# Batch statistics behind the first batch's keys and query, and 16 filler transposes in place of 24, at the start of a gated cross-attention kernel

## The chip, the cores and the metric

The kernel runs on one core of one Trainium2 chip. Its engines are TensorE (PE in the profile, with its weight loads as PEld), VectorE (DVE), ScalarE (ACT), GpSimd (POOL) and SyncE (SP), which issues most DMAs. The metric is the device time of one execution in microseconds; less is better.

## What is computed

Two layers over 8 batches of 112 query tokens of width 256, with 375 context tokens for each batch. Layer 0 is a gated cross-attention with 16 heads of 16, a layer norm for each head on queries and keys, and a feed-forward of three chained matrices; layer 1 is a cross-attention with 8 heads of 64 and a mixture of eight experts. The part that the change lies in is the beginning of layer 0:

```python
x = x + jnp.tanh(g_xattn[0]) * _L0_xattn_ref(_layernorm(x, axis=-1), ctx_1024, Wq, Wkv, Wp, bp, ln_g, ln_b)
# in _L0_xattn_ref
q = (x_query @ Wq).reshape(B, Nq, H, D).transpose(0, 2, 1, 3)
kv = (x_context @ Wkv).reshape(B, Nc, 2, H, D)
q = layernorm(q, ln_g, ln_b)
k = layernorm(k, ln_g, ln_b)
attn = jax.nn.softmax(jnp.einsum('bhqd,bhkd->bhqk', q * SCALE, k), axis=-1)
```

## The kernel before

All five engines run lists of stages that one function, `attention_order`, makes: tables give each stage a due time (in no unit that is measured), all stages are sorted by it, and each engine walks the sorted list and issues the stages that are its own. An engine runs its instructions in that order and waits on semaphores for what other engines deliver. So a changed due time can change the place of a stage on its own engine, and nothing else. The table `FIRST` holds the stages of batches 0 and 1 at the start of layer 0.

Stages that matter here, by the name in the table, the engine and the line of the instruction:

- `stats0` b (VectorE, L1208 and L1210): mean and variance of batch b's tokens, two instructions, BN_STATS and BN_AGGR.
- `rs0` (GpSimd, L2077 into `ve` and L2079 into `rstd`): variance plus epsilon, then the power -1/2. Piece 0 is batch 0; piece 1 is batches 1 and 2 in one instruction each, so it waits for the statistics of both; piece 2 is batches 3 to 7.
- `norm` b (VectorE, L1257): the normalised tokens `XN`; `xt` b (TensorE, L593): their transposes, two of them; `xtc` (ScalarE, L1735) copies them into `XT`.
- `kp` (TensorE, L566, and L610 for the query): products of context and tokens with the key and query weights. One such product in the code is two matmuls in the trace. `kq` (ScalarE, L1801 and L1802): squares into `sq` and the plain copy into `kraw`, which empties the PSUM bank.
- `kss` (VectorE, L1264): sums of squares by head; for batch 0 it is followed by twelve small instructions on VectorE (L1480 to L1491) that find the inverse roots.
- `ksc` (VectorE, L1285): `kraw` times the roots into `KN`, two of them for batch 0; the second holds key third 2 and the query. `qaff` (L1457, VectorE for batch 0) adds the shift to the query.
- `spk` b, j (TensorE, L635, four transposes) turns key third j; `spq` (L643) turns the query. `spkc` (L1523 on VectorE for thirds 0 and 1, L1521 on ScalarE for third 2) and `spqc` (ScalarE, L1820) copy them to `KT0` and `QA0`.
- `S0` q (TensorE, L656): score products of quad q (four heads of one batch), eight matmuls in the trace; `max0` (VectorE, L1295): row maxima; `qt2` (TensorE, L664) and `st` (L674): scores once more, turned; `ex` (ScalarE, L1834): the exponential.
- `v` (TensorE, L566) and `vc` (ScalarE, L1810, into `V`): value products and their copies.

Three PSUM banks are handed round between these products (`take` waits for the copy that empties one): the transposes `spk` 0, 2 need the first of them, `spk` 0, 0 the one that batch 1's first `kq` empties, and `spk` 0, 1 the one that `spkc` 0, 2 empties. The first `kq` of batch 1 may start when the first `ksc` of batch 0 has read `kraw`.

`WARM` names stages ahead of which TensorE runs fillers: transposes of the identity (L559) whose results nobody reads. Ahead of `spk` 0, 2 there are 24.

GpSimd fills buffers (`fill`: `V01`, `KN1`, `ZT`, from 14.09 us on) ahead of piece 1 of `rs0`.

Of the kernel before, what the change touches and what calls it, by code (L numbers as in the profile page):

```python
# [15 lines left out]
NB, NQ, NC, D = 8, 112, 375, 256  # L16
# [70 lines left out]
def emptied_by(stage, *i):  # L87
# [4 lines left out]
    if stage in ("kp", "v"):  # L92
# [13 lines left out]
        (-8.82, 'spkc', 0, 0), (-11.17, 'spk', 0, 1), (-6.18, 'spkc', 0, 1), (-14.74, 'stats0', 1),  # L106
        (-10.6, 'stats0', 2), (-10.72, 'ksc', 0, 0), (-10.44, 'qaff', 0), (-13.38, 'spk', 0, 2),
        (-11.82, 'spkc', 0, 2), (-12.55, 'spq', 0), (-8.21, 'spqc', 0), (-4.49, 'rs0', 1), (9.09, 'rs0', 2),
        (-17.4, 'kp', 1, 1, 0), (-15.19, 'kp', 1, 1, 1), (-13.03, 'kq', 1, 1), (0.4, 'kss', 1, 1),
        (-7.03, 'norm', 1, 0), (-7.61, 'xt', 1, 0), (-6.84, 'xtc', 1, 0), (-10.64, 'kp', 1, 0, 0),  # L110
        (3.62, 'kp', 1, 0, 1), (5.22, 'kq', 1, 0), (8.46, 'kss', 1, 0), (13.34, 'ksc', 1, 1), (17.76, 'spk', 1, 0),
        (17.28, 'spkc', 1, 0), (19.77, 'spk', 1, 1), (18.91, 'spkc', 1, 1), (11.79, 'ksc', 1, 0), (8.26, 'qaff', 1),
        (18.53, 'spk', 1, 2), (16.36, 'spkc', 1, 2), (14.74, 'spq', 1), (15.82, 'spqc', 1))
# [65 lines left out]


RC, RP = 6, 4
WARM = {("kp", 0, 1, 0): 36, ("spk", 0, 2): 24, ("rt4", NB - 1): 14, ("xin", 0): 62,
        ("up", 0, 0): 10}

WARM_BANK = {("up", 0, 0): 5}
# [121 lines left out]
def build(nc, A, out):  # L307
    ctx = ExitStack()
    with ctx:
# [5 lines left out]
        def s(name):  # L315
            if name not in sems:
                sems[name] = ctx.enter_context(nc.semaphore("s_" + name))
            return sems[name]
# [236 lines left out]
        def keep_warm(e, w, *entry):  # L555

            w.wait_ge(s("pool0"), ID_SET)
            for _ in range(WARM.get(entry, 0)):
                e.transpose(ps[:, WARM_BANK.get(entry, 0), 0:128], ident[:, :], ident[:, :])  # L559
# [1875 lines left out]
```

## Time and profile before

| | |
|---|---|
| median of 3 runs | 568.48 us (568.22 to 568.93) |
| profiled execution | 568.3 us, span 566.5 us |
| TensorE busy | 544.5 us, 96% |
| VectorE busy | 392.0 us, 69% |
| ScalarE busy | 318.9 us, 56% |
| GpSimd busy | 224.6 us, 40% |
| granted TensorE clock, mean | 0.996 |

The time of the profiled execution is 1.8 us above its span, which counts from the first to the last instruction. Times in the rows count from the start of the span. "Busy" of TensorE counts pipelined matmuls from start to end, so that a full row of nines does not mean that the array is at its peak. A row of the timeline gives start, duration, engine, line, operation, what it writes and reads, how many were merged into the row, and in brackets how long the engine was idle before it and what released it. In a row of several, the duration reaches from the start of the first to the end of the last.

### The profile page before, as it was taken

What the parts mean: (1) busy time and instruction counts of PE and PEld (TensorE: products, weight loads), DVE (VectorE), ACT (ScalarE), POOL (GpSimd) and SP (SyncE); (2) the same over time, 40 slices, a digit from 0 to 9 for tenths busy, and PEclk for the clock granted to TensorE, in tenths of its full rate; (3) what the DMA queues carried; (4) which work ended last, traced back from release to release, by engine and by line L of the source; (5) the groups of instructions that cost most, each with busy time, mean ns of one, the idle gap of its engine ahead of it and who ended that gap; (6) DMA issues with size and microseconds to landing.
All of it is one profiled execution on the core that took longest, in us unless ns stands there. A gap on an engine that the chain in (4) does not pass through costs nothing.

```text
span 566.5 us, 13539 instructions
## 1 busy us (share of the span) xinstructions
PE 544.5 (96%) x5530; PEld 469.4 (83%) x5530; DVE 392.0 (69%) x764; ACT 318.9 (56%) x629; POOL 224.6 (40%) x239
## 2 busy tenths in 40 slices
PE   8999999999999999999999999999799998999994
PEld 7776767777767878988898888888799996999994
DVE  7887567687778757668765756667676774677752
ACT  3454545655656565666656665556556574567631
POOL 3568549558560134235233432412311333042432
PEclk9999999999999999999999999999999999999998
DMA  8920670000000000000000000007682577177111
GB/s 248 337 94 2 252 311 3 1 3 1 2 2 2 1 1 2 2 9 26 5 23 10 18 17 10 26 1 303 218 276 60 206 262 247 22 256 264 19 12 24
DMA packets 22971, 50.66 MB, mean 89 GB/s; under 512 B 6464, under 2 KB 15728, under 8 KB 19568
## 3 DMA queue, kind: packets, MB, share of 16 engines
q1 hardware_dynamic: 18208, 44.94, 22.2%
q0 software_dynamic: 3456, 3.69, 3.6%
q10 hardware_dynamic: 1232, 1.01, 0.7%
q8 instruction: 49, 0.80, 0.6%
q14 instruction: 26, 0.21, 0.1%
HBM read 37.63 MB, written 12.52 MB: 89 GB/s over the span
## 4 chain that ended last, share of the span: by engine, by line
PE 79%; POOL 8%; DVE 6%; issue 3%; DMA 2%; ACT 1%; POOLq 0%; DVEq 0%
PE ps L65 16%; PE ps L67 15%; PE ps L66 15%; POOL sr L2097 6%; PE ps L799 5%; PE ps L817 5%; PE ps L787 5%; PE ps L656 4%; PE ps L674 3%; DVE KN L1295 3%; PE ps L690 2%; PE ps L635 2%; PE ps L920 1%; PE ps L593 1%; ACT P L1834 1%
## 5 line engine op out<-in xcount | busy, mean ns | idle before, releaser
L2097 POOL TENSOR_TENSOR sr<-sv,mhalf 125x32 f32<-125x32 f32 x13 | 70.6, 5433 | 1.1
L65 PE MATMUL ps<-XGf,WH 128*128 128x256 f32 x252 | 71.0, 282 | 0.0
L66 PE MATMUL ps<-XGf,WH 128*128 128x256 f32 x252 | 71.0, 282 | 0.0
L67 PE MATMUL ps<-XGf,WL 128*128 128x256 f32 x252 | 70.8, 281 | 0.0
L1295 DVE TENSOR_REDUCE KN<-ps 112x4 f32<-112x1500 f32 x32 | 55.0, 1719 | 18.6 <-PE ps L656 18.2
L1710 DVE TENSOR_TENSOR WL<-WR,WH 128x1024 fp32r<-128x1024 f32 x48 | 57.1, 1220 | 12.8 <-ACT WH L2054 8.5
L2170 POOL TENSOR_SCALAR P<-P,rinv 112x487 f32<-112x487 f32 x56 | 40.7, 738 | 56.3 <-DVE rinv L1338 55.3
L1899 ACT ACTIVATE P<-ps,nm 112x487 f32<-112x487 f32 x64 | 42.0, 664 | 23.6 <-DVE nm L1330 23.6
L1834 ACT ACTIVATE P<-ps 125x1344 f32<-125x1344 f32 x32 | 41.4, 1293 | 22.7 <-PE ps L674 22.2
L464 POOL DMA_INDIRECT out<-WS,rows_i x16 | 28.6, 1790 | 62.1 <-ACT WS L1988 46.4
L2054 ACT ACTIVATE WH<-WR 128x1024 fp32r<-128x1024 f32 x48 | 48.8, 1051 | 0.1
L65 PEld LDWEIGHTS ps<-XGf,WH 128*128 128x128 f32 x252 | 47.4, 188 | 0.4 <-issue 0.4
L66 PEld LDWEIGHTS ps<-XGf,WH 128*128 128x128 f32 x252 | 47.4, 188 | 0.0
L67 PEld LDWEIGHTS ps<-XGf,WL 128*128 128x128 f32 x252 | 47.4, 188 | 0.0
L65 PE MATMUL ps<-HTf,CS 128*125 128x256 f32 (+1 forms) x120 | 44.5, 371 | 0.0
L1636 DVE TENSOR_TENSOR P<-P,ps 128x512 f32<-128x512 f32 x32 | 21.9, 686 | 31.2 <-PE ps L67 30.6
L1330 DVE TENSOR_REDUCE nm<-ps 112x1 f32<-112x487 f32 x64 | 38.2, 656 | 4.0 <-PE ps L787 4.0
L1973 ACT ACTIVATE P<-ps 128x512 f32<-128x512 f32 x32 | 19.1, 595 | 37.7 <-PE ps L67 35.7
L67 PE MATMUL ps<-HTf,CS 128*125 128x256 f32 (+1 forms) x120 | 39.2, 327 | 0.0
L65 PE MATMUL ps<-WH,HTf 128*128 128x256 f32 x128 | 36.9, 288 | 0.0
L66 PE MATMUL ps<-WL,HTf 128*128 128x256 f32 x128 | 36.0, 282 | 0.0
L67 PE MATMUL ps<-WH,HTf 128*128 128x256 f32 x128 | 36.0, 281 | 0.0
(302 smaller groups left out, 1502.9 us busy)
## 6 DMA issues: line engine op xcount, KB each, us to landing
WR<-in_gupT SPq DMA_DIRECT2D x16, 1024.0 KB, 7.8
WR<-in_dwnT SPq DMA_DIRECT2D x8, 1024.0 KB, 11.2
xs<-ZT SPq DMA_DIRECT2D x14, 516.0 KB, 6.8
CT<-in_ctxT SPq DMA_DIRECT2D x1, 2250.0 KB, 12.0
P<-xs SPq DMA_DIRECT2D x7, 256.0 KB, 10.5
Wk<-in_L_xattn_Wk SPq DMA_DIRECT2D x2, 512.0 KB, 11.2
Wv<-in_L_xattn_Wv SPq DMA_DIRECT2D x2, 512.0 KB, 11.6
out<-X SPq DMA_DIRECT2D x8, 112.0 KB, 1.9
```

What stands on the lines that cost most here:

```text
L65: e.matmul(out, ah, bh, start=start, stop=False)
L66: e.matmul(out, ah, bl, start=False, stop=False)
L67: return e.matmul(out, al, bh, start=False, stop=stop)
L464: return e.indirect_dma_start(result, rows, src, None, bounds_check=NT - 1, oob_is_err=False, compute_op=ALU.add)
L1295: e.tensor_reduce(heads(KN[b % 2][0:NQ, 3, :])[:, 4 * k:4 * k + 4, 16], ps[0:NQ, 0:4, 0:NC], AX.X, ALU.max, negate=True).then_inc(s("smax" ...
L1330: e.tensor_reduce(nm[:, k:k + 1], ps[0:NQ, scores_bank(*i) + z, 0:487], AX.X, ALU.max, negate=True).then_inc(s("nm"), 1)
L1710: e.tensor_tensor(WL[x % 3][:, cs], WR[x % 3][:, cs], f_(WH[x % 2][:, cs]), ALU.subtract).then_inc(s("wl"), 1)
L1834: e.activation(PQ[:, q % 3, :].rearrange("p (g n) -> p g n", g=4), ps[0:125, 0:4, 0:3 * NQ], ACT.Exp).then_inc(s("ex"), 1)
L1899: e.activation(P[:, k, 0:487], ps[0:NQ, scores_bank(*i) + z, 0:487], ACT.Exp, bias=nm[:, k:k + 1], accum_out=rsum[:, k:k + 1] if i[0] < LA ...
L2054: e.activation(WH[x % 2][:, cs], WR[x % 3][:, cs], ACT.Copy).then_inc(s("wh"), 1)
L2097: e.tensor_tensor(sr[:, p, :], sv[:, p, :], mhalf[0:125, 0:32], ALU.pow).then_inc(s("sr"), 1)
L2170: e.tensor_scalar(P[:, k, 0:487], P[:, k, 0:487], rinv[:, k:k + 1], 1.0, ALU.mult, ALU.mult).then_inc(s("psc"), 1)
```

## The change

Four due times in `FIRST` and one count in `WARM`:

```diff
-        (-8.82, 'spkc', 0, 0), (-11.17, 'spk', 0, 1), (-6.18, 'spkc', 0, 1), (-14.74, 'stats0', 1),
-        (-10.6, 'stats0', 2), (-10.72, 'ksc', 0, 0), (-10.44, 'qaff', 0), (-13.38, 'spk', 0, 2),
+        (-8.82, 'spkc', 0, 0), (-11.17, 'spk', 0, 1), (-6.18, 'spkc', 0, 1), (-10.3, 'stats0', 1),
+        (-8.0, 'stats0', 2), (-10.72, 'ksc', 0, 0), (-10.44, 'qaff', 0), (-13.38, 'spk', 0, 2),
...
-        (-7.03, 'norm', 1, 0), (-7.61, 'xt', 1, 0), (-6.84, 'xtc', 1, 0), (-10.64, 'kp', 1, 0, 0),
+        (-6.1, 'norm', 1, 0), (-6.05, 'xt', 1, 0), (-6.84, 'xtc', 1, 0), (-10.64, 'kp', 1, 0, 0),
...
-WARM = {("kp", 0, 1, 0): 36, ("spk", 0, 2): 24, ("rt4", NB - 1): 14, ("xin", 0): 62,
+WARM = {("kp", 0, 1, 0): 36, ("spk", 0, 2): 16, ("rt4", NB - 1): 14, ("xin", 0): 62,
```

No stage is added or removed, and what each stage does stays the same.

On VectorE, between the last root step of batch 0 and the first row maximum, this stood before (`ksc` is L1285, `qaff` L1457, `stats0` L1208 and L1210, `spkc` L1523, `norm` L1257):

```order
34 L1208 BN_STATS st<-X 112x6
35 L1210 BN_AGGR mv<-st 112x2
36 L1285 TENSOR_TENSOR KN<-kraw,sr 125x32x16 x2
37 L1208 BN_STATS st<-X 112x6
38 L1210 BN_AGGR mv<-st 112x2
39 L1457 TENSOR_TENSOR KN<-KN,S 112x16x16
40 L1523 COPY KT<-ps 128x4x125
41 L1257 TENSOR_SCALAR XN<-X,mv,rstd 112x256
42 L1523 COPY KT<-ps 128x4x125
43 L1257 TENSOR_SCALAR XN<-X,mv,rstd 112x256
44 L1295 TENSOR_REDUCE KN<-ps 112x4
```

and now, in the same place on VectorE:

```order
34 L1285 TENSOR_TENSOR KN<-kraw,sr 125x32x16 x2
35 L1457 TENSOR_TENSOR KN<-KN,S 112x16x16
36 L1208 BN_STATS st<-X 112x6
37 L1210 BN_AGGR mv<-st 112x2
38 L1523 COPY KT<-ps 128x4x125
39 L1208 BN_STATS st<-X 112x6
40 L1210 BN_AGGR mv<-st 112x2
41 L1523 COPY KT<-ps 128x4x125
42 L1257 TENSOR_SCALAR XN<-X,mv,rstd 112x256 x2
43 L1295 TENSOR_REDUCE KN<-ps 112x4
```

Both scalings and the query shift have moved ahead of the statistics of batch 1, the statistics of batch 2 have moved behind the first key copy, and `norm` of batch 1 behind the second.

On TensorE, ahead of the transposes of batch 0's keys, only the number of fillers (L559) differs:

```order
 L610 MATMUL ps<-WS,XT 112x256 x2
 L566 MATMUL ps<-WS,CT 125x256 x10
-L559 MATMUL ps<-ident 128x128 x24
+L559 MATMUL ps<-ident 128x128 x16
 L635 MATMUL ps<-ident,KN 128x125 x8
 L643 MATMUL ps<-ident,KN 128x112 x4
```

Nothing else moves there: `xt` of batch 1 still stands between the key product of batch 1 and the score product of quad 0. The lists of ScalarE, GpSimd and SyncE are as before.

## Rows read from the trace of the kernel before

**Rows 1.** The page, chain that ended last: shares of the span by engine.
```profile
PE 79%; POOL 8%; DVE 6%; issue 3%; DMA 2%; ACT 1%; POOLq 0%; DVEq 0%
```

**Rows 2.** Timeline of TensorE, 15 to 45 us: start us, us, engine, line, operation, idle before.
```profile
15.71 2.78 PE L559 MATMUL ps<-ident 128*128 128x128 f32 x24
18.33 1.02 PE L635 MATMUL ps<-ident,KN 125*128 125x125 f32 x8
...
19.60 0.65 PE L635 MATMUL ps<-ident,KN 125*128 125x125 f32 x4
20.12 1.13 PE L566 MATMUL ps<-WS,CT 128*125 128x256 f32 x4
21.09 0.36 PE L593 MATMUL ps<-ident,XN 112*128 112x112 f32 x2
21.37 0.90 PE L656 MATMUL ps<-KT,QA 32*112 32x375 f32 x8
...
24.12 0.32 PE L664 MATMUL ps<-ident,KN 112*128 112x112 f32 x1 [0.40 <-DVE KN L1295]
```

**Rows 3.** Timeline of VectorE, the same stretch.
```profile
15.87 0.23 DVE L1491 SCALAR_TENSOR_TENSOR sr<-S,sr 125x64 f32<-125x64 f32 x1
16.01 0.42 DVE L1208 BATCH_NORM_STATS2 st<-X 112x6 f32<-112x256 f32 x1
...
16.57 1.27 DVE L1285 TENSOR_TENSOR KN<-kraw,sr 125x512 f32<-125x512 f32 x2
17.76 0.42 DVE L1208 BATCH_NORM_STATS2 st<-X 112x6 f32<-112x256 f32 x1
18.21 0.18 DVE L1210 BATCH_NORM_AGGREGATE mv<-st 112x2 f32<-112x6 f32 x1
18.31 0.41 DVE L1457 TENSOR_TENSOR KN<-KN,S 112x256 f32<-112x256 f32 x1
19.39 0.68 DVE L1523 COPY KT<-ps 128x500 f32<-128x500 f32 x1 [0.67 <-PE ps L635]
19.98 0.40 DVE L1257 TENSOR_SCALAR XN<-X,mv,rstd 112x256 f32<-112x256 f32 x1
20.30 0.67 DVE L1523 COPY KT<-ps 128x500 f32<-128x500 f32 x1
...
22.34 1.72 DVE L1295 TENSOR_REDUCE KN<-ps 112x4 f32<-112x1500 f32 x1 [1.05 <-PE ps L656]
```

**Rows 4.** Timeline of GpSimd, the same stretch.
```profile
18.65 0.23 POOL L2077 TENSOR_SCALAR ve<-mv 112x2 f32<-112x2 f32 x1
18.96 0.72 POOL L2079 TENSOR_TENSOR rstd<-ve,mhalf 112x2 f32<-112x2 f32 x1
```

**Rows 5.** Timeline of ScalarE, the same stretch.
```profile
17.35 0.60 ACT L1801 ACTIVATE sq<-ps 125x512 f32<-125x512 f32 x1 [3.65 <-DVE KN L1285]
17.85 0.59 ACT L1802 ACTIVATE kraw<-ps 125x512 f32<-125x512 f32 x1
18.32 0.60 ACT L1810 ACTIVATE V<-ps 125x512 f32<-125x512 f32 x1
18.96 0.59 ACT L1521 ACTIVATE KT<-ps 128x500 f32<-128x500 f32 x1
```

**Rows 6.** Timeline of all engines, 0 to 40 us: batch 0's `rstd` and `norm`.
```profile
8.27 0.57 POOL L2079 TENSOR_TENSOR rstd<-ve,mhalf 112x1 f32<-112x1 f32 x1
...
8.94 0.41 DVE L1257 TENSOR_SCALAR XN<-X,mv,rstd 112x256 f32<-112x256 f32 x1
```

**Rows 7.** Timeline of all engines, 26.5 to 28.1 us.
```profile
26.60 1.37 POOL L2093 TENSOR_SCALAR sv<-ss 125x32 f32<-125x32 f32 x1
26.97 0.93 DVE L1225 TENSOR_TENSOR CS<-CT,CS 128x750 fp32r<-128x750 f32 x1
```

**Rows 8.** L559's transposes 4.6 to 5.6 (ns min/median/max); TensorE in 72 to 76 us (busy, PEclk).
```profile
L559 PE MATMUL ps<-ident x6: 272/392/421, 4.6 to 5.6; 128*128 128x128 f32 x6
...
72.00:76.00 4.00, 3.04 (x47) 1.00 1.03 399
```

## The prediction

> **What bounds the kernel now.** The chain that ended last gives TensorE (PE) 79% of the span, so most of the kernel is matmul work in a row [rows 1]. The change touches neither that work nor the later stages; it touches the stretch from 16 to 22 us, before the first score product of layer 0. There the question is not who is busy but what the first score product (L656, `S0` of quad 0) waits for, because TensorE runs its list in order and everything later stands behind it. So the views to read are the timelines of the four engines in that stretch, one after the other, with the order of the instructions beside them.
>
> TensorE [rows 2]: 24 fillers from 15.71 us, then eight transposes of keys at 18.33 (thirds 2 and 0), the four of the query, four of keys at 19.60 (third 1), the key product of batch 1 at 20.12, the transposes of batch 1's normalised tokens (L593, `xt`) at 21.09, the score product at 21.37. From 20.12 to 21.37 it has no gap: the score product is held by TensorE's own list. VectorE (DVE) [rows 3]: the last root step ends at 15.87 + 0.23 = 16.10; statistics of batch 1 at 16.01; the two scalings of keys at 16.57, together 1.27; statistics of batch 2 at 17.76, done at 18.21 + 0.18 = 18.39; query shift 18.31; a wait of 0.67 for the transposes; key copy 19.39, `norm` of batch 1 at 19.98, key copy 20.30. GpSimd (POOL) [rows 4]: `ve` 18.65 and the power `rstd` 18.96 to 19.68. So the normalisation that `xt` needs had its input at 19.68, stood behind the key copy until 19.98, and was done at 20.38, 0.7 us before TensorE came to `xt`. That is the slack this change draws on.
>
> After the score product comes a tight chain: it ends at 22.27, the row maximum on VectorE runs 22.34 to 24.06, and the next transpose on TensorE starts at 24.12 [rows 2, 3]. A shift of the first score product is therefore expected to go to the end whole, in either direction: what follows waits for each other's results, not for anything that comes at a fixed time.
>
> **The change, part by part.**
>
> Fillers, 24 to 16. One costs (18.33 - 15.71) / 24 = 0.109 us of TensorE's time [rows 2], eight cost 0.87. The sixteen that stay end at 15.71 + 16 x 0.109 = 17.46. The gain is real only as far as the keys are there.
>
> Key scalings ahead of both statistics. The statistics of batch 1 no longer stand between the root and the scalings. With 0.04 from one instruction's end to the next one that waited for it (the wait of 19.35 to 19.39 [rows 2, 3]), the scalings start at 16.14 and end at 16.14 + 1.27 = 17.41, against 17.84: 0.43 earlier. TensorE can start its key transposes at 17.46, just when the sixteen fillers end. The shortened filler is thus sized to the scalings: 0.87 less on TensorE.
>
> Not all of that 0.87 arrives. ScalarE (ACT) frees two PSUM banks here [rows 5]. Its square of batch 1's first key part started 0.78 after the first scaling (17.35 against 16.57), so now at 16.92; the copy `kraw` follows at 17.42 and ends at 18.01; it frees the bank of the second group of transposes. The first four transposes go 17.46 to 17.89, the second four start at 18.05 and end at 18.05 + 0.59 = 18.64 (half of the eight: 1.02 - 4 x 0.107). The copy to `V` moves to 17.89 and the key copy on ScalarE to 18.37, by ScalarE's own pitch of 0.48 (18.53 if it starts only when the copy to `V` has ended); at 18.96 its bank is free, and the last key transposes start at 19.01 instead of 19.60. The key product of batch 1 then starts at 19.53 and TensorE is at `xt` at 19.53 + 0.97 = 20.50 instead of 21.09. By TensorE alone the first score product would be 0.59 earlier.
>
> Statistics behind the key copy. Count VectorE on: query shift 17.45 to 17.86; statistics of batch 1, a pair that takes 0.55 of the engine (17.76 to 18.31 [rows 3]), 17.77 to 18.39, in what was idle time, so they cost nothing; key copy at 18.68 (transposes done 18.64 + 0.04); after 0.59 (19.39 to 19.98) statistics of batch 2 at 19.27, the second half at 19.72, done at 19.90. Before it was 18.39. These statistics were done 1.5 us earlier, and GpSimd's `rs0` takes both batches in one instruction of two columns, so batch 1's `rstd` waits for batch 2's statistics as well. This is the price of the move. From there: hand-over to GpSimd 0.10 (the same that lies between 8.84, the end of the first `rstd`, and 8.94 [rows 6]), `ve` 20.00, `rstd` 0.31 later at 20.31 and 0.72 long to 21.03 [rows 4], hand-over 0.10, `norm` 21.13 to 21.53 (0.40 [rows 3]), hand-over to TensorE 0.05 (24.06 to 24.12), `xt` at 21.58, score product 0.28 later (21.09 to 21.37) at 21.86. Before: 21.37. **The sum is +0.49 us**: +1.08 at `xt` against TensorE's own new time of 20.50, minus the 0.59 won.
>
> What no row shows is the time of `ve` and `rstd` in their new neighbourhood. Lower bound: both hand-overs at 0.04, which takes 0.12 off: +0.37. Upper bound: if the key transposes and the copy each come by the slower reading (ScalarE's key copy at 18.53, hand-overs of 0.10 throughout), +0.7. I take +0.49. The second key copy on VectorE, 19.82 to 20.50, and `norm` of batch 2, behind `norm` of batch 1, lie beside waits and cost nothing. GpSimd's memsets, which end where `ve` starts before (18.65 [rows 4]), don't move and are no longer what it waits for. SyncE, ScalarE and GpSimd keep their lists, and no DMA is moved.
>
> **Against which time.** The profiled run took 568.3 us, 0.2 below the median of 568.48. The sum gives 568.8 for that run and 568.48 + 0.49 = **568.97** for the median. A measurement of this kernel can tell some 0.2% (1.14 us) from no change: below 567.34 is faster, above 569.62 slower. The forecast is no change that can be told, with the sign on the slow side.
>
> **The rivals.**
>
> (a) The gain at the front wins. If `norm` is there by 20.50, the score product starts at 20.78, -0.59: 567.9. For it: TensorE and ScalarE really are earlier, by rows. Against it: `rstd` would have to be done by about 20.0, before the statistics of batch 2 have even been handed over by the working above. It needs an error of a whole microsecond in a chain of five steps, each with a row.
>
> (b) The shift is absorbed: 568.5. For it: there are waits of several engines later on, and the chain has POOL at 8% [rows 1]. Against it: in the stretch behind the score product the wait of one engine is the work of the next.
>
> (c) Slower, by the GpSimd step. The tiny `sv` at 26.60 took 1.37 while `ve`, as small, takes 0.23; VectorE's subtraction into `CS` ran from 26.97 to 27.90 and `sv` ended with it [rows 7, 4]. One engine can hold the other. In the new order `ve` (20.00) falls into VectorE's key copy (19.82 to 20.50), where it did not before. If that copy holds it as the subtraction held `sv`, it costs up to 1.37 - 0.23 = 1.14 on top: +1.63, 570.1. It decides if `ve` is held beyond some 0.65 us more. Against it: the power at 18.96 ran through the start of the same copy at 19.39 and ended at 19.68, with no sign of it.
>
> The Trainium skill bears on (c) (SBUF — State Buffer, Who interferes with whom): the shared port pair is exclusive, a VectorE instruction with two SBUF inputs contends with a GpSimd one that reads SBUF, and one with at most one SBUF input outside the two-port modes doesn't. By that rule the subtraction holds `sv` and the key copy, whose source is PSUM, does not hold `ve`: the trace agrees for both (1.37, and the power that ended at 19.68), and (c) would fall away; its chance is small for the row's reason alone.
>
> (d) Slower, by TensorE's clock. TensorE now idles from about 20.6 to 21.58 and has lost eight fillers, and if the granted clock falls from 1.00 to a half (2.4 to 1.2 GHz), the products behind run at the slow rate: transposes took 421 ns against 272 on either side of the rise at 4.6 to 5.6 us [rows 8]. Over some 2 us of matmul work that doubles, less what waits anyway, +1.5 to +2: about 570.7. Against it: in the stretch 72 to 76 us TensorE was busy for 3.04 of 4.00 us and the granted clock stayed 1.00 [rows 8], and 20 to 24 will be as busy as that.
>
> A page speaks for a free hand with fillers: the Trainium skill (TensorE: Matmul & The Clock Gate, Part 4) says that transposes don't count as work that raises the clock. Then eight fillers fewer could not matter to (d) at all. The trace differs: only transposes had run when they went from 421 to 272 ns, so fillers do raise it and (d) keeps its chance.
>
> (e) The change doesn't do what it says: the list of VectorE does move, as the order shows, so this can only be that the scalings don't start earlier. Then TensorE waits for them where it ran fillers, and the statistics are as late or later: +0.5 to +0.9, inside the range.
>
> **How the numbers follow.** The late normalisation, with (e): 0.62, 568.8 to 569.4. (b): 0.15, 568.5. (a): 0.12, 567.9, with 0.05 of it for something later that gains too and takes it below 567.34. (c): 0.06, 570.1. (d): 0.05, 570.7. Low end: (a) with a little beyond, 567.8. High end: the upper bound of the main case, 568.48 + 0.7, and the 0.35 to 0.45 by which runs of before stood above the lowest or the median: 569.6. Left out are (c), (d) and a tail of (a), some 0.15. Faster 0.05, slower 0.11, same 0.84.
>
> **What the profile after would show.** Right: key scalings at about 16.1; fillers end at 17.5; key transposes at 17.5 with a short gap before the second four; statistics of batch 2 done at 19.9; `rstd` done at 21.0; a gap of about 1 us on TensorE before `xt`, ended by VectorE's `norm`; the first score product at 21.8 to 21.9; the same lateness at 43 and at the end of the span. Wrong: `xt` at 20.5 with no gap (a); the score product late but the last instructions on time (b); `ve` or `rstd` longer than 0.3 or 0.8 (c); a granted clock under 1.00, or transposes of 421 ns, after 20 us (d).

## The result and the profile after

The changed kernel takes 569.36 us (median of 20 runs, 568.5 to 571.12), the kernel before 568.44 in the same comparison (20 runs, 567.9 to 569.87). The ratio is 1.002, 95% interval 1.0012 to 1.0027: slower by 0.7 to 1.5 us. The forecast was 568.97 and a shift of +0.49. The profiled execution has a span of 567.3 us against 566.5. One of the 12 runs of an experiment below (the kernel before with 16 fillers) took 2928.71 us in a slow state and is left out of its ratio.

Every experiment below is read at the same three points, as a distance from the start of the last root step (the second L1491 of batch 0), since that start moved between 15.54 and 16.67 us from one profile to the next, ahead of all that was edited: to the first score product (first L656), to quad 4's (the L656 near 43 us), and from there to the end of the span.

The timelines of after, in the same columns as before. TensorE, answering [rows 2]:

```profile
15.93 1.91 PE L559 MATMUL ps<-ident 128*128 128x128 f32 x16
17.79 1.15 PE L635 MATMUL ps<-ident,KN 125*128 125x125 f32 x8
18.79 0.60 PE L643 MATMUL ps<-ident,KN 112*128 112x112 f32 x4
19.27 0.65 PE L635 MATMUL ps<-ident,KN 125*128 125x125 f32 x4
19.75 1.09 PE L566 MATMUL ps<-WS,CT 128*125 128x256 f32 x4
21.93 0.39 PE L593 MATMUL ps<-ident,XN 112*128 112x112 f32 x2 [1.09 <-DVE XN L1257]
22.25 0.90 PE L656 MATMUL ps<-KT,QA 32*112 32x375 f32 x8
```

VectorE, answering [rows 3]:

```profile
16.09 0.22 DVE L1491 SCALAR_TENSOR_TENSOR sr<-S,sr 125x64 f32<-125x64 f32 x1
16.35 1.29 DVE L1285 TENSOR_TENSOR KN<-kraw,sr 125x512 f32<-125x512 f32 x2
17.68 0.42 DVE L1457 TENSOR_TENSOR KN<-KN,S 112x256 f32<-112x256 f32 x1
18.02 0.42 DVE L1208 BATCH_NORM_STATS2 st<-X 112x6 f32<-112x256 f32 x1
18.48 0.18 DVE L1210 BATCH_NORM_AGGREGATE mv<-st 112x2 f32<-112x6 f32 x1
18.98 0.68 DVE L1523 COPY KT<-ps 128x500 f32<-128x500 f32 x1 [0.32 <-PE ps L635]
19.58 0.42 DVE L1208 BATCH_NORM_STATS2 st<-X 112x6 f32<-112x256 f32 x1
20.03 0.18 DVE L1210 BATCH_NORM_AGGREGATE mv<-st 112x2 f32<-112x6 f32 x1
20.13 0.65 DVE L1523 COPY KT<-ps 128x500 f32<-128x500 f32 x1
21.37 0.73 DVE L1257 TENSOR_SCALAR XN<-X,mv,rstd 112x256 f32<-112x256 f32 x2 [0.60 <-POOL rstd L2079]
23.22 1.72 DVE L1295 TENSOR_REDUCE KN<-ps 112x4 f32<-112x1500 f32 x1 [1.11 <-PE ps L656]
```

GpSimd, answering [rows 4]:

```profile
20.30 0.23 POOL L2077 TENSOR_SCALAR ve<-mv 112x2 f32<-112x2 f32 x1 [1.40 <-DVE mv L1210]
```

ScalarE, the plain copy that frees a PSUM bank, answering [rows 5]:

```profile
17.65 0.59 ACT L1802 ACTIVATE kraw<-ps 125x512 f32<-125x512 f32 x1
```

TensorE by stretches (busy time, matmuls, granted clock, share of the DMA engines, GB/s), with the gap in them:

```profile
19.00:21.00 2.00, 1.84 (x12) 1.00 1.12 274
21.00:23.00 2.00, 1.07 (x10) 1.00 1.12 299
```

Read from the end: the score product follows `xt`, `xt` waited 1.09 us for `norm` (XN L1257), `norm` 0.60 for GpSimd's `rstd`, and GpSimd 1.40 for the statistics of batch 2 (mv L1210). TensorE had ended all that stands ahead of `xt` at 20.84 (21.93 - 1.09), so its own list was indeed ahead. The first score product stands 6.16 us behind the last root step, against 21.37 - 15.87 = 5.50 [rows 2, 3]: **+0.66**. At quad 4 it is 28.01 against 27.35, again +0.66.

### The profile page after: what moved, and what is told of

Its sections match the earlier page's. It is cut to its first block, busy times and chain, and to the rows that moved or that the text cites. A ratio compares the mean times of both kernels' runs of the same rounds, so it can differ in the third digit from the quotient of the medians.

```text
span 567.3 us, 13523 instructions
## 1 busy us (share of the span) xinstructions
PE 544.3 (96%) x5522; PEld 469.3 (83%) x5522; DVE 392.6 (69%) x764; ACT 318.7 (56%) x629; POOL 224.8 (40%) x239
## 3 DMA queue, kind: packets, MB, share of 16 engines
q0 software_dynamic: 3456, 3.69, 3.5%
## 4 chain that ended last, share of the span: by engine, by line
PE 82%; POOL 8%; DVE 6%; issue 2%; ACT 1%; DMA 1%; POOLq 0%
PE ps L65 16%; PE ps L67 15%; PE ps L66 15%; POOL sr L2097 6%; PE ps L799 5%; PE ps L817 5%; PE ps L787 5%; PE ps L656 4%; PE ps L674 3%; DVE KN L1295 3%; PE ps L690 2%; PE ps L635 2%; PE ps L559 2%; PE ps L566 1%; PE ps L920 1%
```

## The experiments

All kernels in one table, in us. Distances come from one profile each; the third column is a span, known to 0.1, less a start. The ratios come from timed runs beside the kernel before. None of them is a difference of 2%; an interval that leaves out 1 shows a direction and little more.

| kernel | first score product | quad 4 | from quad 4 to the end | ratio to before, 95% |
|---|---|---|---|---|
| before | 5.50 | 27.35 | 523.3 | |
| after | 6.16 | 28.01 | 523.2 | 1.002 (1.0012 to 1.0027) |
| after again | 6.15 | 28.01 | 523.5 | 1.0009 (0.9996 to 1.0021) |
| before, 16 fillers | 5.29 | 27.15 | 523.6 | 1.0 (0.9989 to 1.0011) |
| after, 24 fillers | 6.78 | 28.64 | 523.5 | 1.0031 (1.0013 to 1.0049) |
| before, 33 fillers | 6.48 | 28.33 | 523.4 | 1.0018 (1.0003 to 1.0034) |
| after, both statistics first | 5.33 | 27.18 | 523.2 | 0.9998 (0.9989 to 1.0008) |
| after, `rstd` one batch each | 5.47 | 27.33 | 523.5 | 1.0002 (0.9994 to 1.0011) |
| after, `xt` behind the score product | 4.74 | 26.93 | 523.6 | 0.9987 (0.9978 to 0.9996) |
| both statistics first, `xt` behind | 4.77 | 26.78 | 523.4 | 0.9985 (0.9976 to 0.9994) |
| the same again | 4.78 | 26.79 | 523.3 | 0.9989 (0.998 to 0.9998) |
| the same, weight split later | 4.78 | 27.23 | 523.4 | 1.0003 (0.9994 to 1.0013) |
| the same, no fillers there | 4.78 | 26.78 | 526.6 | 1.0044 (1.0026 to 1.0061) |
| the same, the fillers moved to 403 us | 4.78 | 26.78 | 524.9 | 1.0016 (1.0005 to 1.0028) |

### The changed kernel again

No edit; it shows how much of a difference between comparisons is chance.

> The changed kernel once more. In its profile the whole beginning lay 0.2 us later than in the profile before (last root step 16.09 against 15.87), ahead of anything that the change moves; the rest of the lateness of the first score product, 0.67 us, lies behind it. Theory (late normalisation): the offset of the beginning is chance and goes, the distance from the last root step to the first score product stays at 6.1 to 6.2 us (5.50 before), and the kernel is 0.6 to 0.8 us slower than before. Rival (something beyond that stretch also costs): the distance is the same but the kernel is 1.0 to 1.4 us slower.

Measured: the distances repeat to 0.01 us (6.15, 28.01), while the median, 569.02, and the ratio (0.5 us; 0.6 to 0.8 was forecast) are lower than in the first comparison. In the 20 runs of the first, seven lay at 570.2 or above, six of these with a mean granted clock of 0.994 or 0.995 where all the others had 0.996 to 0.998; here two of 12 lay so high, both at 0.994. So the medians carry about half a microsecond that has nothing to do with the order at 16 us, and mechanisms are better read from the distances.

### The two halves of the change, each alone

Only the fillers, on the kernel before:

```diff
-WARM = {("kp", 0, 1, 0): 36, ("spk", 0, 2): 24, ("rt4", NB - 1): 14, ("xin", 0): 62,
+WARM = {("kp", 0, 1, 0): 36, ("spk", 0, 2): 16, ("rt4", NB - 1): 14, ("xin", 0): 62,
```

> The kernel before with 16 fillers in place of 24, its due times as they were. Theory: TensorE is ready at about 17.5 and waits for the key scalings that end at 17.84; the banks that ScalarE empties hold it a little more; the first score product comes 0.1 to 0.3 us earlier than before and the time is 568.2 to 568.4, no difference that can be told. Rival (the fillers carry the clock): the granted clock falls or the transposes go to 421 ns after 16 us, and the kernel is 1 to 2 us slower.

Measured: -0.21 at the first score product, and no difference in time (1.0). Eight fillers, worth 0.87 of TensorE's time, gain only 0.2 as long as the key scalings stand behind the statistics: TensorE idles 0.37 for them. The rival, that the fillers carry the clock, fails here: granted clock 1.00 from 15 to 25 us, transposes of 270 ns.

Only the order, with 24 fillers left (the same line, from 16 back to 24 in the kernel after):

> The changed kernel with 24 fillers: the new order alone. Theory: the fillers hold the key transposes to their old time, the first key copy on VectorE with them, and the statistics of batch 2 behind it end at 20.6; rstd at 21.7, the first score product 1.3 us later than before, 0.6 later than with 16 fillers: 569.7 to 569.9. Rival (the statistics are not what the score product waits for): 568.4 to 569.0.

Measured: +1.28 (1.3 forecast), and 570.03 us. The later transposes push the key copy on VectorE to 19.49, behind it the statistics of batch 2 (20.09 and 20.54), and `ve`, which waits for them:

```profile
19.49 0.68 DVE L1523 COPY KT<-ps 128x500 f32<-128x500 f32 x1 [0.95 <-PE ps L635]
20.09 0.42 DVE L1208 BATCH_NORM_STATS2 st<-X 112x6 f32<-112x256 f32 x1
20.54 0.18 DVE L1210 BATCH_NORM_AGGREGATE mv<-st 112x2 f32<-112x6 f32 x1
...
20.81 0.23 POOL L2077 TENSOR_SCALAR ve<-mv 112x2 f32<-112x2 f32 x1 [2.02 <-DVE mv L1210]
```

The halves don't add (-0.21 and +1.28 against +0.66 together), because in the new order the fillers also set the time of the key copy behind which the statistics stand.

### Does a shift pass to the end?

Nine fillers more than before, 33, cost 0.98 us of TensorE's time and touch nothing else.

```diff
-WARM = {("kp", 0, 1, 0): 36, ("spk", 0, 2): 24, ("rt4", NB - 1): 14, ("xin", 0): 62,
+WARM = {("kp", 0, 1, 0): 36, ("spk", 0, 2): 33, ("rt4", NB - 1): 14, ("xin", 0): 62,
```

> The kernel before with 33 fillers in place of 24: nine more transposes, 0.98 us, and nothing else. It measures how much of a lateness of the first score product reaches the end. Theory (all of it): the distance from the last root step to the first score product is 5.50 + 0.98 = 6.5 us, the rest of the run stays at 545.0 to 545.4 us after the start of that product, the time is 0.9 to 1.1 us above before. Rival (part is absorbed later): the rest of the run is shorter by 0.3 us or more, the time rises by less than 0.6.

Measured: +0.98 at the first score product, +0.98 at quad 4, 523.4 from there to the end, ratio 1.0018 (+1.0 us, with an interval from 0.2 to 1.9; the medians differ by 0.5). By the profile, lateness passes one to one. That rules out rival (b). For a gain it is not shown by this run, and further below a part of one is lost.

### What makes `norm` late

First the place of batch 2's statistics: back ahead of the key copy, all else as changed.

```diff
-        (-8.0, 'stats0', 2), (-10.72, 'ksc', 0, 0), (-10.44, 'qaff', 0), (-13.38, 'spk', 0, 2),
+        (-10.2, 'stats0', 2), (-10.72, 'ksc', 0, 0), (-10.44, 'qaff', 0), (-13.38, 'spk', 0, 2),
```

> The changed kernel with the statistics of batch 2 ahead of the first key copy, right behind those of batch 1; 16 fillers. Theory: they end at 19.0 in place of 20.0, the first key copy starts 0.1 to 0.2 us later, norm is no longer held by rstd; the first score product comes 0.2 to 0.4 us earlier than in the kernel before and 0.9 to 1.1 earlier than in the changed one: 568.1 to 568.3. Rival (the loss lies elsewhere, in the fillers or the scalings): stays at 569.1 to 569.4.

Measured: the loss is gone, -0.17 against before and 0.83 less than in after, each just short of the forecast (0.2 to 0.4 and 0.9 to 1.1); the median, 568.64, is that of the kernel before. `ve` starts at 19.05 here, and TensorE still idles 0.17 ahead of `xt`, since `norm` now waits for VectorE's second key copy:

```profile
18.77 0.18 DVE L1210 BATCH_NORM_AGGREGATE mv<-st 112x2 f32<-112x6 f32 x1
...
19.05 0.23 POOL L2077 TENSOR_SCALAR ve<-mv 112x2 f32<-112x2 f32 x1 [0.38 <-DVE mv L1210]
...
20.87 0.38 PE L593 MATMUL ps<-ident,XN 112*128 112x112 f32 x2 [0.17 <-DVE XN L1257]
```

Then the coupling of the two batches: statistics where the change puts them, but GpSimd's step split, so that batch 1's `rstd` doesn't wait for batch 2's statistics.

```diff
-        (-11.82, 'spkc', 0, 2), (-12.55, 'spq', 0), (-8.21, 'spqc', 0), (-4.49, 'rs0', 1), (9.09, 'rs0', 2),
+        (-11.82, 'spkc', 0, 2), (-12.55, 'spq', 0), (-8.21, 'spqc', 0), (-4.49, 'rs0', 1), (-4.48, 'rs0', 2), (9.09, 'rs0', 3),
...
-                        w.wait_ge(s("rstd0"), (2, 4, 4, 6, 6, 6, 6, 6)[b])
+                        w.wait_ge(s("rstd0"), (2, 4, 6, 8, 8, 8, 8, 8)[b])
...
-                    bs = slice((0, 1, 3)[i[0]], (1, 3, NB)[i[0]])
+                    bs = slice((0, 1, 2, 3)[i[0]], (1, 2, 3, NB)[i[0]])
```

> The changed kernel with the GpSimd step for batches 1 and 2 in two: one ve and one rstd for batch 1, then the same for batch 2. Batch 1 no longer waits for the statistics of batch 2, whose place on VectorE stays behind the first key copy. Theory: the first rstd is done at about 19.6 us, norm of batch 1 starts right behind the second key copy at 20.4, the first score product 0.1 to 0.2 us earlier than before by distance from the last root step (5.3 to 5.4 us), 0.8 less than in the changed kernel; 568.3 to 568.6. Rival (it is the place of the statistics on VectorE, not the shared step, that costs): the distance stays at 6.1.

Measured: 5.47 (5.3 to 5.4 forecast), so the loss of 0.66 is gone with this edit as well. Batch 1's `rstd` was done at 19.40; its `norm` now waited for VectorE itself and started at 20.34, right behind the second key copy:

```profile
18.82 0.58 POOL L2079 TENSOR_TENSOR rstd<-ve,mhalf 112x1 f32<-112x1 f32 x1
...
20.34 0.93 DVE L1257 TENSOR_SCALAR XN<-X,mv,rstd 112x256 f32<-112x256 f32 x2
```

So the late `norm` is what costs, and its cause is both together: batch 2's statistics behind the key copy, and one GpSimd step for both batches. Undoing either is enough.

### Does the score product have to wait for `xt` at all?

The score product of batch 0 needs nothing from batch 1's tokens; `xt` only stands ahead of it in the list. Here `xt` and its copy are due later, once on the changed kernel and once with both statistics first.

```diff
-        (-6.1, 'norm', 1, 0), (-6.05, 'xt', 1, 0), (-6.84, 'xtc', 1, 0), (-10.64, 'kp', 1, 0, 0),
+        (-6.1, 'norm', 1, 0), (-0.5, 'xt', 1, 0), (-2.5, 'xtc', 1, 0), (-10.64, 'kp', 1, 0, 0),
```

> The changed kernel with those two transposes behind the first score product, the late statistics left where they are. Theory: the score product starts 4.9 to 5.1 us after the last root step in place of 6.16, since it no longer stands behind the late normalisation; the transposes (at 5.8) and what hangs on them then hold qt2, which lands near its distance in the kernel before, and most of the loss is gone: 568.3 to 568.7. Rival (the late normalisation costs the same wherever it is waited for): 569.0 to 569.4.

> The kernel with both statistics ahead of the first key copy (16 fillers), and the two transposes of batch 1's normalised tokens placed behind the first score product on TensorE instead of ahead of it. Theory: the score product then waits only for the second key copy and TensorE's own list, and starts 4.9 to 5.0 us after the last root step (5.50 before, 5.33 with the statistics alone moved); but the key product of batch 1's query and the copy between stand behind it, so the transpose qt2 comes 0.3 to 0.5 us earlier than before, not 0.6; 568.0 to 568.3, the fastest of all. Rival (the gain is lost on the way to qt2): qt2 at the old distance, the same time as with the statistics alone moved.

Measured: on the changed kernel `norm` is as late as in after (`ve` 20.28, `norm` 21.36), and nobody waits for it ahead of the score product:

```profile
20.28 0.23 POOL L2077 TENSOR_SCALAR ve<-mv 112x2 f32<-112x2 f32 x1 [1.39 <-DVE mv L1210]
...
20.81 0.90 PE L656 MATMUL ps<-KT,QA 32*112 32x375 f32 x8
21.36 0.74 DVE L1257 TENSOR_SCALAR XN<-X,mv,rstd 112x256 f32<-112x256 f32 x2 [0.60 <-POOL rstd L2079]
```

The distance falls to 4.74, 0.76 below before; the ratios are 0.9987 and 0.9985. Both came out better than forecast (4.9 to 5.1 and 4.9 to 5.0). The late `norm` is not wholly free there: quad 4 lies at 26.93 against 26.78 with both statistics first. In that second kernel the first L664 comes 0.74 earlier than before (7.51 against 24.12 - 15.87 = 8.25), and 0.57 is left at quad 4, so a gain did not pass whole. Its next row maximum on VectorE (24.43) stood behind a weight split (L1243) that itself waited 0.23 for ScalarE:

```profile
23.82 0.69 DVE L1243 TENSOR_TENSOR XGf<-WS,HTf 128x512 fp32r<-128x512 f32 x1 [0.23 <-ACT HTf L1794]
24.43 1.71 DVE L1295 TENSOR_REDUCE KN<-ps 112x4 f32<-112x1500 f32 x1
```

If the split is what held it, putting it later should give the 0.17 back:

```diff
-WEIGHTS = ((2.33, 'wkv', 0), (26.73, 'wkv', 1), (148.95, 'w2', 0), (149.57, 'w2', 1), (164.61, 'w1', 0),
+WEIGHTS = ((5.8, 'wkv', 0), (26.73, 'wkv', 1), (148.95, 'w2', 0), (149.57, 'w2', 1), (164.61, 'w1', 0),
```

> The fastest order so far, and the split of the first half of the key-value weights (L1794 on ScalarE, L1243 on VectorE) due behind the second row maximum instead of ahead of it. In that order's trace the second row maximum started at 24.43, held by this step on VectorE, which waited 0.23 for ScalarE, and the 0.74 us won at qt2 had shrunk to 0.57. Theory (won back in full): the second maximum starts 0.16 us earlier, the product of quad 4 comes 26.6 us after the last root step, 567.7. Rival (a new wait): the split and the context split now stand between the second maximum and the roots of batch 1, which end 0.4 us later and hold the third maximum; quad 4 at 26.9 to 27.2, 568.0 to 568.3.

It didn't. The second maximum did come earlier (8.74 behind the last root step, 8.89 without the edit), but the split then ran behind it, ahead of the sums of squares, and the roots and the third maximum came later (30.92, a distance of 14.89; 14.49 without the edit): quad 4 at 27.23, 1.0003. The split costs its time on VectorE somewhere, and its first place was the better one.

The version with both statistics first and `xt` behind, once more, without an edit:

> The fastest order so far once more (statistics first, transposes behind the score product, 16 fillers), to see whether it beats the kernel before: it measured 0.9985 of it. Theory: the distances within the first 45 us repeat to 0.05 us (quad 4 at 26.78), the kernel is 0.5 to 0.9 us faster than before, 567.8 to 568.1. Rival (that measurement was high): within 0.3 us of before.

Measured: 4.78 and 26.79, 568.12 us, 0.9989 (0.998 to 0.9998). Twice the interval lies below 1: this version is faster than the kernel before, by 0.6 and 0.9 us (the two intervals reach from 0.1 to 1.4). It was not timed beside the changed kernel; its distance at quad 4 is 1.23 shorter than that one's.

### Are the fillers worth anything?

In that version the sixteen fillers cover the wait for the key scalings. Without them:

```diff
-WARM = {("kp", 0, 1, 0): 36, ("spk", 0, 2): 16, ("rt4", NB - 1): 14, ("xin", 0): 62,
+WARM = {("kp", 0, 1, 0): 36, ("rt4", NB - 1): 14, ("xin", 0): 62,
```

> The fastest order so far (statistics first, the two transposes behind the score product) with no filler at all ahead of the key transposes. TensorE then idles from about 15.4 to 17.3 us. It tells whether the fillers carry anything but time. Theory (they only hide in a wait): the key transposes start when the scalings are done, the first score product at the same 4.8 us after the last root step, the granted clock stays 1.00, the time is that of the kernel with 16 fillers, 567.9. Rival (they carry the clock): after the idle time the products behind run at the slow rate, the distance to the product of quad 4 (26.78 us) grows by 1 us or more, 569 or above.

Measured: the first 45 us agree with and without them (4.78, 26.78), though TensorE now idles 1.70 ahead of the key transposes. Its timeline and its stretches there, without the fillers:

```profile
17.86 1.15 PE L635 MATMUL ps<-ident,KN 125*128 125x125 f32 x8 [1.70 <-DVE KN L1285]
```

```profile
15.00:17.00 2.00, 1.17 (x6) 1.00 1.02 423
17.00:19.00 2.00, 1.14 (x9) 1.00 0.98 385
```

The granted clock stays 1.00 across the gap. And yet the time is 570.61, 1.0044 (11 runs from 568.85 to 573.93, so one profile doesn't tell how often what follows happens). In the profile all of it is lost 390 us later, where TensorE waits for rows that GpSimd has scattered to memory and that a load brings back (P<-xs). GpSimd's last scatter, the issue of the load, and the transposes that wait for it, without the fillers:

```profile
404.83 0.94 POOL L2180 DMA_INDIRECT xs<-S,pos  x1 [0.30 <-issue]
409.46 0.33 SPq L2317 DMA_DIRECT2D P<-xs  x1
...
412.06 1.11 PE L966 MATMUL ps<-ident,P 128*128 128x128 f32 x4 [3.72 <-DMA P<-xs]
```

and with them:

```profile
404.18 0.94 POOL L2180 DMA_INDIRECT xs<-S,pos  x1 [0.30 <-issue]
406.77 0.33 SPq L2317 DMA_DIRECT2D P<-xs  x1
...
409.41 0.66 PE L966 MATMUL ps<-ident,P 128*128 128x128 f32 x4 [1.72 <-DMA P<-xs]
```

From the end of the scatter's issue to the load it takes 409.46 - 405.77 = 3.69 us instead of 1.65, and TensorE idles 3.72 instead of 1.72. Towards the end of that longer gap the granted clock (the number behind the count) begins to fall, behind it it is a half, and the four transposes take 1.11 instead of 0.66:

```profile
408.00:410.00 2.00, 0.34 (x4) 1.00 0.02 4
410.00:412.00 2.00, 0.00 (x0) 0.88 0.65 158
412.00:414.00 2.00, 1.94 (x9) 0.50 0.80 127
414.00:416.00 2.00, 2.00 (x16) 0.77 0.42 8
416.00:420.00 4.00, 4.00 (x36) 1.00 0.92 282
```

The loss has two parts. By distance from quad 4 the waiting transposes start 2.03 later (412.06 - 42.94 against 409.41 - 42.32), which is the late landing; from them to the end it takes 157.4 instead of 156.3, which is what the slower clock behind the gap can account for.

Does the late landing belong to the fillers' absence at 16 us, or to the length of TensorE's program up to there? The sixteen fillers are put ahead of the transposes that wait:

```diff
-WARM = {("kp", 0, 1, 0): 36, ("spk", 0, 2): 16, ("rt4", NB - 1): 14, ("xin", 0): 62,
+WARM = {("kp", 0, 1, 0): 36, ("rt4", NB - 1): 14, ("xin", 0): 78,
```

> The fastest version (both statistics first, transposes of batch 1's tokens behind the first score product) without the 16 fillers ahead of the key transposes, and with 78 in place of 62 fillers ahead of the late transposes that wait for the scattered rows, so that TensorE's program is as long as before. Without the 16 early ones alone, the first 45 us were the same, and the late wait for the scattered rows grew from 1.72 to 3.72 us, with the granted clock falling behind it. Sixteen more there are 16 x 0.109 = 1.75 us. Theory A, the early fillers are of no worth and the late wait comes from where or how long TensorE's program is: the loads are issued some 1.65 us behind the end of the last scatter's issue again, the idle time ahead of the late transposes is at most 0.3 us, the clock stays 1.00 there, quad 4 at 26.8 us behind the last root step, 567.6 to 568.1. Theory B, what delays the landing is that TensorE has less to do at 16 us: loads again 3.7 us behind, idle time about 2 us, 569 to 570. If neither: the loads 1.65 us behind and idle time left all the same, then the fillers hide nothing and the wait isn't made of the landing.

Measured: 569.7 us, 1.0016. The landing is nearly as late (405.83 to 409.19, 3.36 us), so theory A fails in its main point, and theory B's numbers (3.7, about 2, 569 to 570) lie nearer. With the sixteen fillers there the idle time is 1.59, the clock is 1.00 from 406 to 420 us, and from the transposes to the end it takes 156.2 again. So the second part of the loss is gone and the first is not:

```profile
411.73 0.66 PE L966 MATMUL ps<-ident,P 128*128 128x128 f32 x4 [1.59 <-DMA P<-xs]
```

The view of the DMA queues shows what lies in the way. A row gives packets, megabytes, and their time as a share of 16 engines. In this kernel with the fillers moved, 406.4 to 406.6 us, while the last scatter's data move:

```profile
q0 software_dynamic: 12, 0.05, 87.6%
q8 instruction: 1, 0.02, 45.6%
```

and 407.8 to 409.2:

```profile
q0 software_dynamic: 3, 0.01, 3.0%
```

The one packet of the instruction queue took 0.456 x 16 x 0.2 = 1.46 us, so it ended at about 408.0. All but three of the scatter's packets (queue 0) were through by 407.1; those three came from 408.0 on, and the waiters were released at 409.19. In the kernel before, the packet lies two scatters earlier (404.0 to 404.2):

```profile
q0 software_dynamic: 12, 0.05, 89.2%
q8 instruction: 1, 0.02, 46.0%
```

and its last scatter is complete by 407.2, released at 407.62. Where the packet falls goes with the fillers ahead of the key transposes. Its start, against the end of the last scatter's issue, is -2.7 us with 33 fillers, -1.9 with 24 (both kernels), -1.1 to -1.2 with 16 (all nine), and +0.7 (fillers moved) and +1.5 (none) without. With 16 or more, the last scatter was always released 1.64 to 1.85 us after its issue; without, after 3.36 and 3.69. So the likely cause is an instruction fetch that slid into the last scatter because TensorE's program is shorter ahead of it. The kernel without fillers shows the same pattern: the packet ends at 408.3, and the last three of the scatter's come from 408.3 on. But this is read from traces and not shown: no view tells which DMA engine a packet is on or whose instructions it carries, and no run moved the fetch alone. Two things fit badly. The packet of the kernel without fillers is recorded as starting at 407.3, 0.3 us after all but three of the scatter's. And that kernel and the one with the fillers moved differ by 0.8 in the packet's place, though they have the same instructions up to the fillers ahead of the waiting transposes, among which the packet falls. This part stays open.

## Why the prediction was right, and where its working was off

**The bound.** Right for the way it went: the first score product was late by what held `xt`, and the lateness arrived whole at quad 4 and at the end (33 fillers: +0.98 at both points, and the rest as long as before). "In either direction" is more than the runs bear out: of the 0.74 won at the first L664 with `xt` moved, 0.57 was left at quad 4.

**TensorE's own gain.** Right. The forecast had batch 1's key product at 19.53 - 15.87 = 3.66 behind the last root step, and it came at 19.75 - 16.09 = 3.66; with the 0.97 from it to `xt` in the kernel before, TensorE could have been at `xt` at 4.63, as forecast. (20.84 is the end of the last product of that row, 1.09 long; two neighbours overlap, so in this count TensorE is ready 0.12 later.) One hand-over on the way was off: the scalings ended at 16.35 + 1.29 = 17.64 and the first transpose started at 17.79, 0.15 later, where 0.05 had been taken. It cost nothing, because the second group of transposes waited for the bank that `kraw` empties, as forecast: `kraw` ended at 18.24, and a timeline cut at 18.42 shows the fifth transpose starting at 18.30, 2.21 behind the last root step where 2.18 was forecast. The short gap ahead of it lies inside the row of eight, which takes 1.15 instead of 1.02.

**Statistics behind the key copy: the price.** Right in kind, shown by two different cures (5.33 and 5.47 against 6.16). Forecast for `ve` 20.00 - 15.87 = 4.13, measured 4.21: the transposes that the first key copy waits for ended 0.08 later than computed (18.94 - 16.09 = 2.85 against 2.77), since their second group took longer than half of the old row. For `norm` the forecast was 5.26 and the measurement 5.28, and that closeness is in part luck: GpSimd's hand-over to VectorE took 0.04 where 0.10 had been taken, which hides most of the 0.08.

**The mis-sized term** is the last hand-over to TensorE. `norm` ended at 21.37 + 0.41 = 21.78, and `xt` started at 21.93: 0.15, where the prediction took 0.05 from the row maximum and the next transpose. And `xt` to the score product took 0.32 where it took 0.28. Together 0.14 of the 0.17 that lie between +0.49 and +0.66. How long TensorE had idled doesn't explain the 0.15: it had idled for 0.40 both ahead of the row that gave 0.05 and ahead of `xt` with `rstd` one batch each, where the hand-over was 0.15 again. What does is open. The stated upper bound, +0.7, held the 0.66, with some luck as well: it allowed 0.10 for each hand-over, this one took more and the one from GpSimd less; and ScalarE's slower key copy, which it also names, doesn't lie on the way to `norm`.

**Rival (a)** did not happen: TensorE and ScalarE were earlier, but `norm` was not there, and TensorE stood ready 1.09 before it could start `xt`. **Rival (b)**: ruled out by the 33 fillers. **Rival (c)**: `ve` took 0.23 us inside the key copy (20.30, with the copy from 20.13 to 20.78), no longer than outside of one [rows 4]; the subtraction that held `sv` is not what this copy is. The rule quoted from the Trainium skill (SBUF — State Buffer, Who interferes with whom) agrees with both. **Rival (d)** did not happen at 20 us, granted clock 1.00 through a gap of 1.09, and not even with no fillers at all and a gap of 1.70 at 16 us. But its mechanism is real elsewhere: at 410 us, with a gap of 3.72, the clock fell to 0.50. **Rival (e)**: the scalings did start earlier, 0.26 behind the last root step against 0.70 [rows 3].

**The time.** The profile's span moved by +0.8, of which 0.22 is the later start and 0.66 the mechanism. The medians differ by 0.92 in the first comparison and 0.4 in the second, where the interval of the ratio reaches below 1. So the median of 569.36, 0.39 above the forecast, holds 0.17 of the mis-sized terms, and the rest is in part the seven high runs of that comparison. The forecast of "no change that can be told", with the sign on the slow side, held by its own bound of 1.14 us; the first interval leaves out 1, so 20 runs can sometimes tell less than that.

## What to carry to other kernels

When a step is moved behind another one to free the front, look for who shares an instruction with it: here batch 1 paid for batch 2's statistics because one GpSimd step took both. Before trimming a wait, ask whether the instruction that waits has to stand there at all; moving `xt` behind the score product took 1.08 us off the changed kernel's way to quad 4, and the better order of what it waited for took 0.83. And in the kernels without the fillers at 16 us, a load near 408 us landed late, for a cause that is open: read the rest of the span too, not only the place of the edit.

## What was not expected of the hardware

- TensorE started 0.15 us after the end of the VectorE instruction that it waited for in some places, and 0.06 after it in others, whatever it had idled before. 0.15: at 17.79 and 21.93 in after (idle 1.09 ahead of the second), ahead of `xt` with both statistics first (0.17) and with `rstd` one batch each (0.40), ahead of the key transposes without fillers (1.70). 0.06: at 24.12 in the kernel before (0.40), and ahead of `xt` at 21.83 in the changed kernel with `xt` behind (0.12). Among the others, VectorE to GpSimd took 0.09 (20.21 to 20.30), GpSimd to VectorE 0.04 (21.33 to 21.37).
- One 16 KB packet of instructions took 1.0 to 1.5 us, and in the two profiles where it started behind the last scatter's issue, that scatter was released 1.5 to 2.0 us later than in the other twelve.
- The granted clock stayed 1.00 through a gap of 1.70 us at 16 us and through one of 1.59 at 410 us, and fell to 0.50 with one of 3.72 at 410 us.
